# Attention on one core: half of the first image's pixels projected from whole fp32 values

## The chip, the cores and the metric

The kernel runs on one core of a Trainium2 chip. The metric is the device time of one execution in microseconds (us); lower is better.

## What is computed

Four images of 256 channels and 32 x 32 = 1024 pixels go through one attention layer. With x of one image as a 256 x 1024 matrix:

```python
q = einsum('oc,bcn->bon', Wq, xf) + bq      # 32 x 1024
k = einsum('oc,bcn->bon', Wk, xf) + bk      # 32 x 1024
v = einsum('oc,bcn->bon', Wv, xf) + bv      # 256 x 1024
attn = softmax(einsum('bqi,bqj->bij', q, k), axis=-1)
out = einsum('bcj,bij->bci', v, attn) + x
```

All tensors are fp32.

## The kernel before

**Parts.** Every fp32 operand of a matmul is cut in two: a high part of reduced precision (`x_hi`, `wqk_hi`, `wv_hi`, `v_hi`, `w_hi`, type fp32r) and the rest (`..._lo`, the value less its high part). A product is made of three matmuls into the same accumulator: high x high, low x high, high x low. Low x low is left out.

**Stages of an image.** q and k are projected together, one accumulator of 512 columns for each half of the pixels (`qk_home`); the scores of eight tiles of 128 queries are made for their row maxima and exponential sums (`first_scores`, `scores`; maxima on VectorE in `row_max`, L665, exponentials on ScalarE in `sum_exp`, L500); v is projected in eight tiles of 128 pixels x 256 channels (`v_tile`, L939); then a loop of 16 steps makes the transposed weights (`scores_t`) and multiplies v with them (`weigh_v`). In that loop the front stages of the next image are laid between the steps. The channels are two blocks of 128 (CT = 2), so each projection adds up two blocks.

**Start.** For the first image there is nothing to lay its front stages beside. The order of TensorE is written out by hand (L1078 to L1101): twenty matmuls on zeros (`keep_busy`), the q, k projection in four pieces (`first_project_qk`; piece i is channel block i // 2 and pixel half i % 2), v tiles 0 and 1, scores 0 to 2, v tiles 2 and 3, score 3, v tiles 4 and 5, the rows of shifts (`first_rows`), v tiles 6 and 7 around the first two transposed scores, then the loop, which begins with the first weighting matmul (L1009). Waits between engines are semaphores that each instruction raises when it ends; each engine runs its instructions in the order written.

**Who feeds the start.** SP's queue loads x of image 0 in two channel blocks (L278), then `wv` (L279), and after `wv` has landed x of image 1. ScalarE's queue loads `small` (L485): the q and k weights, the biases of q and k, and the bias of v. ScalarE cuts x into `x_hi` in four pieces (L487 to L490) and then `wv` into `wv_hi` (L569), and puts k and part of q with their bias (`put_k_hi`, `put_q_hi`, `put_q2_full`). VectorE cuts the weights of q and k (L624, L626) from a source that repeats each block of 32 twice, so that the accumulator holds k, k, q, q in its 128 partitions, makes `x_lo` (L632), then puts the first quarter of q (L769) and the low parts of q and k (`put_q_lo`, `put_k_lo`), then takes the four row maxima. GpSimd copies each block of the cut weights once into `wqk_pair` (L416 to L421), which the projections of images 1 to 3 use; makes `wv_lo` (L424); copies two quarters of q (`put_q_dup`); cuts and splits the second half of q (`split_q2`); then cuts and splits x of image 1 and splits the first weight tiles (`split_w`). Score 0 waits for k's low parts, q's low part and the first q copy; score 1 for q's second low part; score 2 for the second q copy; score 3 for the first exponential, since it is written over score 0; v tile 4 for the second exponential.

## Time and profile before

| | us |
|---|---|
| median of 3 executions | 163.77 |
| lowest and highest | 163.71 and 164.1 |
| the profiled execution | 163.81 |
| its span, first to last instruction | 162.0 |
| TensorE matmul busy | 157.5 (97%) |
| VectorE busy | 133.9 (83%) |
| ScalarE busy | 109.2 (67%) |
| GpSimd busy | 60.0 (37%) |

The span is counted from the first instruction recorded to the last; the execution's time holds some 1.8 us outside it. A matmul's length in a timeline includes the passage through the array, so neighbours overlap; the distance between two starts is what one costs in a row of them. The number behind an x is a count of instructions, and a bracket at the end of a row gives idle time ahead of it and what ended it. Line numbers (L849) are those of the kernel before. TensorE's operands are listed as result <- moving, stationary or the reverse, by the program's names; a product of `v_tile` is listed at L849, the line of its helper `group`, or at L948 and L952 for tile 0.

### The profile page before, as it was taken

The page shows a single profiled execution, that of the slowest core. Times are in us where ns is not written, and L with a number is a line of the kernel's source. Part 1 is how long each engine was busy: PE and PEld are TensorE (multiplying, and loading weights), DVE is VectorE, ACT ScalarE, POOL GpSimd, SP SyncE. Part 2 cuts the span into 40 slices and gives each one's busy share as a digit, 9 for nine tenths or more (in the row PEclk, how much of TensorE's full clock was granted, in tenths as well). Part 3 has the DMA queues.
Part 4 walks back from the last instruction along what each step waited for, and adds up shares of the span by engine and source line. Part 5 has one row for each costly group of instructions (what it writes and reads, how often), then busy time and mean ns, then how long its engine had stood idle before and what let it go on. Part 6 is the DMA issues. An engine that isn't in the chain of part 4 may idle for free.

```text
span 162.0 us, 2456 instructions
## 1 busy us (share of the span) xinstructions
PE 157.5 (97%) x788; PEld 132.3 (82%) x788; DVE 133.9 (83%) x215; ACT 109.2 (67%) x200; POOL 60.0 (37%) x68
## 2 busy tenths in 40 slices
PE   7999999999999999999999999999999999999993
PEld 5677887798888887798888897788888898888882
DVE  1899998888988989997989989895989779846952
ACT  3679887969999545827999646736896655756400
POOL 4479946256222316348443300342333300124500
PEclk9999999999999999999999999999999999999999
DMA  4576672152103030162711130162320330003003
GB/s 161 187 299 166 243 235 89 31 151 63 55 0 97 1 129 2 37 144 67 268 39 49 54 129 0 37 146 67 121 61 1 97 129 0 0 5 129 0 0 130
DMA packets 7780, 14.67 MB, mean 91 GB/s; under 512 B 1504, under 2 KB 2072, under 8 KB 7768
## 3 DMA queue, kind: packets, MB, share of 16 engines
q1 hardware_dynamic: 6728, 13.46, 25.4%
q0 software_dynamic: 608, 0.80, 2.2%
q10 hardware_dynamic: 432, 0.26, 0.5%
q8 instruction: 6, 0.10, 0.3%
q14 instruction: 6, 0.05, 0.1%
HBM read 4.79 MB, written 4.20 MB: 55 GB/s over the span
## 4 chain that ended last, share of the span: by engine, by line
PE 90%; DMA 2%; ACT 2%; DVE 2%; issue 1%; DVEq 0%
PE acc L1009 32%; PE acc L1015 16%; PE slot L849 11%; PE st L996 9%; PE slot L909 7%; PE slot L1009 5%; DMA small_sb<-small 2%; PE slot L1015 2%; ACT dump L504 2%; PE slot L861 2%; PE slot L866 2%; PE slot L935 1%; DVE negmax L667 1%; PE slot L881 1%; DVE x_lo L632 0%
## 5 line engine op out<-in xcount | busy, mean ns | idle before, releaser
L402 POOL TENSOR_TENSOR w_lo<-w_full,w_hi 128x512 fp32r<-128x512 f32 x21 | 28.0, 1338 | 46.6 <-ACT w_full L542 25.4
L1009 PE MATMUL acc<-w_hi,v_hi 128*128 128x512 f32 x112 | 44.3, 395 | 0.0
L1009 PE MATMUL acc<-w_hi,v_lo 128*128 128x512 f32 x112 | 44.1, 394 | 0.0
L542 ACT ACTIVATE w_full<-st 128x512 f32<-128x512 f32 x62 | 36.8, 594 | 7.6 <-PE st L996 7.5
L504 ACT ACTIVATE dump<-slot,negmax 128x1024 f32<-128x1024 f32 x29 | 32.5, 1119 | 10.5 <-DVE negmax L667 10.1
L667 DVE TENSOR_REDUCE negmax<-slot 128x1 f32<-128x1024 f32 x29 | 35.2, 1217 | 2.7 <-PE slot L909 2.7
L1015 PE MATMUL acc<-w_lo,v_hi 128*128 128x512 f32 x112 | 37.4, 396 | 0.0
L734 DVE TENSOR_TENSOR w_lo<-w_full,w_hi 128x512 fp32r<-128x512 f32 x43 | 30.7, 719 | 3.6 <-issue 0.5
L1009 PEld LDWEIGHTS acc<-w_hi,v_hi 128*128 128x128 f32 x112 | 21.1, 189 | 5.0 <-issue 0.2
L1009 PEld LDWEIGHTS acc<-w_hi,v_lo 128*128 128x128 f32 x112 | 21.2, 189 | 4.8
L1015 PEld LDWEIGHTS acc<-w_lo,v_hi 128*128 128x128 f32 x112 | 21.0, 188 | 4.8
L996 PE MATMUL st<-q_b,k_b 98*128 98x512 f32 x62 | 24.5, 398 | 0.1
L725 DVE CAST w_hi<-w_full 128x512 fp32r<-128x512 f32 x40 | 19.5, 489 | 3.0 <-ACT w_full L542 1.5
L539 ACT ACTIVATE w_hi<-st 128x512 fp32r<-128x512 f32 x24 | 14.3, 594 | 6.2 <-PE st L996 6.0
L849 PE MATMUL slot<-wv_hi,x_hi 128*128 128x256 f32 x62 | 17.4, 281 | 0.4 <-ACT dump L504 0.4
L849 PE MATMUL slot<-wv_lo,x_hi 128*128 128x256 f32 x62 | 17.4, 281 | 0.0
L849 PE MATMUL slot<-wv_hi,x_lo 128*128 128x256 f32 x62 | 17.3, 280 | 0.0
L909 PE MATMUL slot<-k_a,q_a 96*128 96x512 f32 x48 | 15.2, 397 | 0.0
L531 ACT ACTIVATE v_hi<-slot 128x512 fp32r<-128x512 f32 x12 | 7.2, 599 | 11.8 <-PE slot L849 11.8
L265 POOL DMA_DIRECT2D q_b<-shift_rows x7 | 4.2, 602 | 29.5 <-DVE shift_rows L706 27.0
L715 DVE TENSOR_TENSOR v_lo<-slot,v_hi 128x512 fp32r<-128x512 f32 x16 | 11.0, 690 | 3.8 <-ACT v_hi L531 3.7
L909 PEld LDWEIGHTS slot<-k_a,q_a 96*128 96x128 f32 x48 | 13.0, 310 | 1.1
(102 smaller groups left out, 225.2 us busy)
## 6 DMA issues: line engine op xcount, KB each, us to landing
out<-x_sb SPq DMA_DIRECT2D x7, 512.0 KB, 2.8
x_sb<-x SPq DMA_DIRECT2D x3, 1024.0 KB, 5.1
k_b<-k_a SPq DMA_DIRECT2D x8, 192.0 KB, 2.6
q_b<-q_a SPq DMA_DIRECT2D x8, 192.0 KB, 2.6
x_sb<-x SPq DMA_DIRECT2D x2, 512.0 KB, 4.2
k_a<-qk_parts SPq DMA_DIRECT2D x12, 64.0 KB, 2.0
q_a<-qk_parts SPq DMA_DIRECT2D x12, 64.0 KB, 2.2
k_a<-qk_parts POOLq DMA_DIRECT2D x6, 64.0 KB, 2.2
```

Source lines behind the costliest of these rows:

```text
L402: nc.gpsimd.tensor_tensor(w_lo[:, r, :], w_full[:, r, :], w_hi[:, r, :].bitcast(fp32), ALU.subtract).then_inc(w_split_pool, 1)
L504: nc.scalar.activation(dump[:, t % 2, :], s_home(b, t), ACT.Exp, bias=negmax[:, t:t + 1], accum_out=rowsum[:, t:t + 1]).then_inc(rowsum_re ...
L539: nc.scalar.activation(w_hi[:, r, :], st_home(n), ACT.Exp).then_inc(w_cut_act, 1)
L542: nc.scalar.activation(w_full[:, r, :], st_home(n), ACT.Exp).then_inc(exp_done, 1)
L667: nc.vector.tensor_reduce(out=negmax[:, t:t + 1], in_=s_home(b, t), op=ALU.max, axis=AX.X, negate=True).then_inc(negmax_ready, 1)
L725: nc.vector.tensor_copy(w_hi[:, r, :], w_full[:, r, :]).then_inc(w_cut_dve, 1)
L734: nc.vector.tensor_tensor(w_lo[:, r, :], w_full[:, r, :], w_hi[:, r, :].bitcast(fp32), ALU.subtract).then_inc(w_split_dve, 1)
L849: last = nc.tensor.matmul(dst, lhs, rhs, start=(i == 0), stop=(i == len(terms) - 1))
L909: last = nc.tensor.matmul(s_home(b, t)[:, cols(h)], pixels(b, t), k_a[0:K_A, cols(h)], start=True, stop=True)
L996: nc.tensor.matmul(st_home(n), k_b[0:K_B, j * P:(j + 1) * P], q_b[0:K_B, cols(h)], start=True, stop=True).then_inc(st_ready, 1)
L1009: nc.tensor.matmul(dst, v[:, b % 2, j, c * P:(c + 1) * P], w_hi[:, n % RING, part], start=(j == 0 and v is v_hi), stop=False)
L1015: return nc.tensor.matmul(dst, v_hi[:, b % 2, j, c * P:(c + 1) * P], w_lo[:, n % RING, part], start=False, stop=(j == JT - 1))
```

## The change

For the first half of the first image's pixels, q, k and v are projected by matmuls whose operands are the uncut fp32 tensors `x_sb`, `small_sb` and `wv`: one for each channel block instead of three. The second half of its pixels and all other images keep their parts; ScalarE and VectorE cut and split x of image 0 for the second pixel half only (two pieces of 512 columns each instead of four). The weights of q and k lie in `small` as k, k, q (96 columns for each channel block instead of 64), and `wqk_hi` and `wqk_lo` are 96 columns wide instead of 128. `wqk_pair` is now made by GpSimd from `small_sb` by a copy and a subtraction, behind `x0_split`; the first q copy goes ahead of `wv_lo` in GpSimd's order. TensorE runs 18 zero matmuls instead of 20, waits for `small`, takes whole and cut products in turn (block 0 whole, block 0 parts, block 1 whole, block 1 parts), waits for `wv` in place of its high part ahead of v tile 0, and for `wv_lo` ahead of v tile 4. `add_bias` on ScalarE, in the loop, waits for the v tiles of image 0 in place of its splits.

```diff
-        small_sb = sb("small_sb", [P, CT * 2 * CQK + 2 + CT])
-        bias = small_sb[:, CT * 2 * CQK:CT * 2 * CQK + 2]
-        bv_sb = small_sb[:, CT * 2 * CQK + 2:CT * 2 * CQK + 2 + CT]
-        wqk_hi = sb("wqk_hi", [P, CT, P], fp32r)
-        wqk_lo = sb("wqk_lo", [P, CT, P], fp32r)
+        KKQ = 3 * CQK
+        small_sb = sb("small_sb", [P, CT * KKQ + 2 + CT])
+        bias = small_sb[:, CT * KKQ:CT * KKQ + 2]
+        bv_sb = small_sb[:, CT * KKQ + 2:CT * KKQ + 2 + CT]
+        wqk_hi = sb("wqk_hi", [P, CT, KKQ], fp32r)
+        wqk_lo = sb("wqk_lo", [P, CT, KKQ], fp32r)
...
-            for half, (parts, made) in enumerate(((wqk_hi, wqk_cut), (wqk_lo, wqk_split))):
-                pool.wait_ge(made, 1)
-                nc.gpsimd.tensor_copy(
-                    wqk_pair[:, :, half * 2 * CQK:(half + 1) * 2 * CQK].rearrange("p c (g r) -> p c g r", g=2),
-                    parts[:, :, :].bitcast(fp32).rearrange("p c (g d r) -> p c g d r", g=2, d=2)[:, :, :, 0, :],
-                ).then_inc(pair_made, 1)
+            wqk = small_sb[:, 0:CT * KKQ].rearrange("p (c g r) -> p c g r", c=CT, g=3)[:, :, 0:3:2, :]
+
+            def pair(half):
+                return wqk_pair[:, :, half * 2 * CQK:(half + 1) * 2 * CQK].rearrange("p c (g r) -> p c g r", g=2)
+
+            pool.wait_ge(small_in, DMA)
+
+            pool.wait_ge(x0_split, CT)
+            nc.gpsimd.tensor_copy(pair(HI), wqk).then_inc(pair_made, 1)
+            pool.wait_ge(pair_made, 1)
+            nc.gpsimd.tensor_tensor(pair(LO), wqk, pair(HI).bitcast(fp32), ALU.subtract).then_inc(pair_made, 1)
             pool.wait_ge(pair_made, 2)
+            put_q_dup(0)
+            pool.wait_ge(q_dup_put, 1)
             pool.wait_ge(wv_cut, 1)
             nc.gpsimd.tensor_tensor(wv_lo[:, :, :], wv[:, :, :], wv_hi[:, :, :].bitcast(fp32),
                                     ALU.subtract).then_inc(wv_split, 1)
             pool.wait_ge(wv_split, 1)
-            put_q_dup(0)
-            pool.wait_ge(q_dup_put, 1)
             put_q_dup(1)
...
             act.preload_act_table_set("natural_log_exp_and_others")
-            for i in range(4):
-                c, part = piece(i)
+
+            for c in range(CT):
                 act.wait_ge(x0_in[c], DMA)
-                nc.scalar.activation(x_hi[:, 0, c, part], x_sb[:, 0, c, part], ACT.Copy).then_inc(x0_cut, 1)
-
+                nc.scalar.activation(x_hi[:, 0, c, cols(1)], x_sb[:, 0, c, cols(1)], ACT.Copy).then_inc(x0_cut, 1)
...
-                act.wait_ge(x0_split, 4)
+
+                act.wait_ge(v_ready, 4)
...
             dve.wait_ge(small_in, DMA)
-
-
-            def twice(w):
-                return w[:, :, :].rearrange("p c (g d r) -> p (c g) d r", g=2, d=2)
-
-            wqk = small_sb[:, 0:CT * 2 * CQK].rearrange("p (g o r) -> p g o r", o=1, r=CQK)
-            wqk = wqk.broadcast_to([P, CT * 2, 2, CQK])
-            nc.vector.tensor_copy(twice(wqk_hi), wqk).then_inc(wqk_cut, 1)
+            wqk = small_sb[:, 0:CT * KKQ].rearrange("p (c w) -> p c w", c=CT)
+            nc.vector.tensor_copy(wqk_hi[:, :, :], wqk).then_inc(wqk_cut, 1)
             dve.wait_ge(wqk_cut, 1)
-            nc.vector.tensor_tensor(twice(wqk_lo), wqk, twice(wqk_hi).bitcast(fp32),
+            nc.vector.tensor_tensor(wqk_lo[:, :, :], wqk, wqk_hi[:, :, :].bitcast(fp32),
                                     ALU.subtract).then_inc(wqk_split, 1)
-
-            for i in range(4):
-                c, part = piece(i)
-                dve.wait_ge(x0_cut, i + 1)
-                nc.vector.tensor_tensor(x_lo[:, 0, c, part], x_sb[:, 0, c, part],
-                                        x_hi[:, 0, c, part].bitcast(fp32), ALU.subtract).then_inc(x0_split, 1)
+            for c in range(CT):
+                dve.wait_ge(x0_cut, c + 1)
+                nc.vector.tensor_tensor(x_lo[:, 0, c, cols(1)], x_sb[:, 0, c, cols(1)],
+                                        x_hi[:, 0, c, cols(1)].bitcast(fp32), ALU.subtract).then_inc(x0_split, 1)
...
-            def first_project_qk(i):
-                c, part = piece(i)
-                dst = qk_home(0, i % 2)
-                if i == 0:
-                    pe.wait_ge(wqk_cut, 1)
-                pe.wait_ge(x0_cut, i + 1)
-                nc.tensor.matmul(dst, wqk_hi[:, c, :], x_hi[:, 0, c, part], start=(c == 0), stop=False)
-                if i == 0:
-                    pe.wait_ge(wqk_split, 1)
-                nc.tensor.matmul(dst, wqk_lo[:, c, :], x_hi[:, 0, c, part], start=False, stop=False)
-                pe.wait_ge(x0_split, i + 1)
-                last = nc.tensor.matmul(dst, wqk_hi[:, c, :], x_lo[:, 0, c, part], start=False, stop=(c == CT - 1))
+            def first_project_whole(c):
+
+                pe.wait_ge(x0_in[c], DMA)
+                last = nc.tensor.matmul(qk_home(0, 0)[0:KKQ, :], small_sb[:, c * KKQ:(c + 1) * KKQ], x_sb[:, 0, c, cols(0)],
+                                        start=(c == 0), stop=(c == CT - 1))
+                if c == CT - 1:
+                    last.then_inc(qk_ready, 1)
+
+            def first_project_parts(c):
+
+                dst = qk_home(0, 1)[0:KKQ, :]
+                pe.wait_ge(wqk_cut, 1)
+                pe.wait_ge(x0_cut, c + 1)
+                nc.tensor.matmul(dst, wqk_hi[:, c, :], x_hi[:, 0, c, cols(1)], start=(c == 0), stop=False)
+                pe.wait_ge(wqk_split, 1)
+                nc.tensor.matmul(dst, wqk_lo[:, c, :], x_hi[:, 0, c, cols(1)], start=False, stop=False)
+                pe.wait_ge(x0_split, c + 1)
+                last = nc.tensor.matmul(dst, wqk_hi[:, c, :], x_lo[:, 0, c, cols(1)], start=False, stop=(c == CT - 1))
...
             def v_tile(b, t):
                 px = slice(t * P, (t + 1) * P)
                 dst = v_home(b, t // VT)[:, t % VT * C:(t % VT + 1) * C]
-                terms = [(xs[:, b % 2, c, px], w[:, c, :]) for c in range(CT)
-                         for xs, w in ((x_hi, wv_hi), (x_hi, wv_lo), (x_lo, wv_hi))]
-                if b == 0 and t == 0:
-
-                    for c in range(CT):
-                        for xs in (x_hi, x_lo):
-                            nc.tensor.matmul(dst, xs[:, 0, c, px], wv_hi[:, c, :],
-                                             start=(c == 0 and xs is x_hi), stop=False)
-                    pe.wait_ge(wv_split, 1)
-                    for c in range(CT):
-                        nc.tensor.matmul(dst, x_hi[:, 0, c, px], wv_lo[:, c, :], start=False, stop=(c == CT - 1))
-                    return
+                if b or t >= TH:
+                    terms = [(xs[:, b % 2, c, px], w[:, c, :]) for c in range(CT)
+                             for xs, w in ((x_hi, wv_hi), (x_hi, wv_lo), (x_lo, wv_hi))]
+                else:
+                    terms = [(x_sb[:, 0, c, px], wv[:, c, :]) for c in range(CT)]
                 last = group(dst, terms)
...
-            keep_busy(20, QUARTER)
-            for i in range(4):
-                first_project_qk(i)
-            pe.wait_ge(wv_cut, 1)
+            keep_busy(18, QUARTER)
+            pe.wait_ge(small_in, DMA)
+            for c in range(CT):
+                first_project_whole(c)
+                first_project_parts(c)
+            pe.wait_ge(wv_in, DMA)
...
             pe.wait_ge(rowsum_ready, 2)
+            pe.wait_ge(wv_split, 1)
             v_tile(0, 4)
...
-            by_partition(np.concatenate([wk, wq], axis=0)),
+            by_partition(np.concatenate([wk, wk, wq], axis=0)),
```

## Rows read from the trace of the kernel before

**Rows 1.** Page: the span; busy time and share of TensorE.
```profile
span 162.0 us, 2456 instructions
...
PE 157.5 (97%) x788; PEld 132.3 (82%) x788; DVE 133.9 (83%) x215; ACT 109.2 (67%) x200; POOL 60.0 (37%) x68
```

**Rows 2.** By stretch: length, busy each engine, granted clock, DMA share, GB/s.
```profile
5.27:5.70 0.43, 0.43 (x3) 0.43 (x2) 0.43 (x2) 0.38 (x1) 0.43 (x2) 1.00 1.04 405
...
18.97:162.00 143.03, 140.25 (x696) 119.16 (x694) 119.77 (x191) 96.17 (x179) 46.86 (x47) 1.00 0.24 73
```

**Rows 3.** Chain of work that ended last, 0 to 26 us: start, length, what.
```profile
0.75 3.94 DMA small_sb<-small
...
11.17 1.24 DVE negmax L667
```

**Rows 4.** Timeline of PE, 0 to 23 us: start, length, line, operation, operands, count.
```profile
1.06 4.45 PE L1076 MATMUL st<-idle 128*128 128x256 bf16 x20 [1.06 <-DVE idle L614]
5.27 0.59 PE L876 MATMUL slot<-x_hi,wqk_hi 128*128 128x512 f32 x1
5.70 0.40 PE L879 MATMUL slot<-x_hi,wqk_lo 128*128 128x512 f32 x1
...
7.72 0.39 PE L881 MATMUL slot<-x_lo,wqk_hi 128*128 128x512 f32 x1
...
8.64 0.28 PE L948 MATMUL slot<-wv_hi,x_hi 128*128 128x256 f32 x1
...
10.32 0.81 PE L935 MATMUL acc<-k_a,q_a 96*128 96x512 f32 x2
...
12.18 0.28 PE L849 MATMUL slot<-wv_hi,x_hi 128*128 128x256 f32 x1
...
13.47 0.28 PE L849 MATMUL slot<-wv_hi,x_lo 128*128 128x256 f32 x1
13.69 0.74 PE L935 MATMUL acc<-k_a,q_a 96*128 96x512 f32 x2
14.82 0.38 PE L849 MATMUL slot<-wv_hi,x_hi 128*128 128x256 f32 x1 [0.39 <-ACT dump L504]
...
18.97 0.47 PE L1009 MATMUL acc<-w_hi,v_hi 128*128 128x512 f32 x1
...
22.79 0.63 PE L1015 MATMUL acc<-w_lo,v_hi 128*128 128x512 f32 x2
```

**Rows 5.** Timeline of PEld, TensorE's weight loads, 0 to 12 us.
```profile
9.50 0.19 PEld L849 LDWEIGHTS slot<-wv_hi,x_hi 128*128 128x128 f32 x1
```

**Rows 6.** Timeline of DVE, 0 to 22 us.
```profile
5.38 2.68 DVE L632 TENSOR_TENSOR x_lo<-x_sb,x_hi 128x512 fp32r<-128x512 f32 x4
8.15 0.48 DVE L769 TENSOR_SCALAR q_a<-slot,small_sb 32x256 fp32r<-32x256 f32 x1
...
9.18 1.40 DVE L642 SCALAR_TENSOR_TENSOR k_a<-slot,small_sb,k_a 32x512 fp32r<-32x512 f32 x2
...
14.57 1.22 DVE L667 TENSOR_REDUCE negmax<-acc 128x1 f32<-128x1024 f32 x1
```

**Rows 7.** Timeline of ACT, 0 to 22 us.
```profile
4.50 1.15 ACT L490 ACTIVATE x_hi<-x_sb 128x512 fp32r<-128x512 f32 x2 [2.04 <-DMA x_sb<-x]
5.82 1.15 ACT L490 ACTIVATE x_hi<-x_sb 128x512 fp32r<-128x512 f32 x2 [0.17 <-DMA x_sb<-x]
...
15.82 1.12 ACT L504 ACTIVATE dump<-acc,negmax 128x1024 f32<-128x1024 f32 x1
```

**Rows 8.** Timeline of POOL, 0 to 22 us.
```profile
5.14 0.47 POOL L418 CAST wqk_pair<-wqk_hi 128x128 fp32r<-128x128 f32 x1 [2.30 <-DVE wqk_hi L624]
...
20.92 1.29 POOL L402 TENSOR_TENSOR w_lo<-w_full,w_hi 128x512 fp32r<-128x512 f32 x1 [0.23 <-ACT w_full L542]
```

**Rows 9.** Issues of the DMA queues: issue, KB each, median us to landing.
```profile
x_sb<-x SPq DMA_DIRECT2D x2, 512.0 KB, 4.2
...
small_sb<-small ACTq DMA_DIRECT2D x1, 66.0 KB, 3.9
```

More of the change, by code:

```diff
@@ L122, in nonlocal_attention @@
         wqk_split = sem("wqk_split")
+        x0_cut = sem("x0_cut")
+        x0_split = sem("x0_split")
         pair_made = sem("pair_made")
@@ L125, in nonlocal_attention @@
         wv_split = sem("wv_split")
-        x0_cut = sem("x0_cut")
-        x0_split = sem("x0_split")
         x1_cut = sem("x1_cut")
```

## The prediction

> **What bounds the kernel now.** The first view is the busy table of the page: TensorE's matmuls cover 97% of a span of 162.0 us [rows 1]. The second is the busy time by stretch: from the first weighting matmul at 18.97 us to the end they are busy 140.25 of 143.03 us, and the change touches nothing in that stretch but one GpSimd order [rows 2]. So the time can move only by the start of that stretch, and what counts is what sets 18.97. The chain of waits tells it for the stretch before [rows 3]: the transfer of `small`, the projection of q and k on TensorE, VectorE's conversions of the first scores operands, then from 11.17 four row maxima on VectorE and four exponentials on ScalarE, back to back. The last exponential starts at 15.82 [rows 7] just behind the last maximum, which runs from 14.57 to 15.79 [rows 6]; everything up to 18.97 hangs on it. VectorE has its score 3 at 13.69 + 0.74 = 14.43, 0.14 ahead of 14.57 [rows 4, 6].
>
> **Unit prices.** Two full-speed paces come from TensorE's timeline [rows 4]. Four starts from 7.72 to 8.64 give 0.23 us for a product of 512 columns; eleven from 12.18 to 13.47 give 0.117 for one of 256. Early on the pace is slower: 20 idle products of 256 columns between 1.06 and 5.27 make 0.21 each, and the first real product holds the array from 5.27 to 5.70, 0.43 for 512 columns. That is the 1.2 GHz level, and from 5.70 on the pace is that of the 2.4 GHz level, although the granted clock of the first, slow stretch is printed as 1.00 [rows 2].
>
> **The price that no row shows** is that of a multiply on whole 32-bit values: all matmuls of the trace are on parts or on bf16 zeros. From below it is one product of its columns (0.23 or 0.117). The nearest rows are the three products of parts that it replaces (0.69 or 0.35). Two values cut in two have four products; the kernel leaves out low times low, a whole multiply can't. I take four products, 0.92 and 0.47, as the likely value. From above I let a weight load, 0.19 us long [rows 5], come bare on top of each whole multiply: 1.11 and 0.66.
>
> The Trainium skill (FP8 and Floating Point Precision, TensorE Precision Notes) gives true FP32 four passes through the array, which is the value taken. Another page of the Trainium skill (Perfetto Trace Analysis, Engine Utilization) halves the array's output rate for FP32_LOW_HIGH; read as the rate of a whole multiply, that would make it two products, the third rival below. No trace here shows either.
>
> **Part 1, q and k of image 0.** Removed are six products of parts of the first pixel half, added two whole multiplies: 12 products become 6 + 8 = 14. Two idle products go, so real work can start at 1.06 + 18 x 0.21 = 4.85 instead of 5.27. It then needs `small` and the first half of x. `small` has landed at 0.75 + 3.94 = 4.69 [rows 3], ScalarE starts on x at 4.50 [rows 7]. `small` grows from 132 to 196 columns, 66 to 98 KB. At the 405 GB/s of the stretch [rows 2] 33 KB more are 0.08 us. A 512 KB transfer landed in 4.2 us against 3.9 for this one [rows 9], so size costs little: 0 to 0.3, I take 0.08, and it hides in the 0.16 between 4.69 and 4.85. At 0.3 TensorE would start 0.14 later at the slow pace, 0.07 lost. From 4.85 to 5.70 the slow pace makes (5.70 - 4.85) / 0.43 = 2 products, the other 12 take 12 x 0.23 = 2.76, and the v tiles start at 8.46 instead of 8.64. The first half is ready when the second whole multiply drains: three products before 8.46, plus 0.16 (0.39 long less 0.23 of pace), so 7.93 against 7.72 + 0.39 = 8.11. The second half moves as much. That is 0.18 earlier for both.
>
> What feeds the second half stays behind this: ScalarE cuts two pieces instead of four, from 4.50 and, with the landing of the second half of x, from 5.82, each in some 0.6 [rows 7], and VectorE's subtraction takes 2.68 / 4 = 0.67 [rows 6], so x_lo of the second piece is there at 5.82 + 0.6 + 0.67 = 7.1, and TensorE asks for it at 8.46 - 0.23 = 8.23. Fewer weight columns (96 for 128) change no pace, since pace goes by the moving columns. The weight conversions on VectorE get shorter and wait for nothing new; they cost nothing, and are needed only from 4.85 + 0.85 + 0.46 = 6.16.
>
> **Part 2, VectorE's chain.** It started at 8.15 on the first half's projection [rows 6] and now starts at 7.97. Its second k conversion ended at 9.18 + 1.40 = 10.58, now 10.40.
>
> **Part 3, v tiles 0 and 1.** Twelve products become four whole multiplies, 16 products: 16 x 0.117 = 1.87, from 8.46 to 10.33. Before they took 8.64 to 10.32, which held a short wait for wv_lo that goes away. Score 0's first product thus starts as before; its second follows the k conversion as it did, 0.16 behind it (10.32 + 0.81 - 0.39 = 10.74 against 10.58), so at 10.56. The first row maximum moves from 11.17 to 10.99, and scores 1 and 2 move along: the next v tiles start at 12.18 - 0.18 = 12.00.
>
> **Part 4, v tiles 2 and 3.** Again 16 products for 12: 12.00 + 1.87 = 13.87. Before, score 3 came at 13.69, held by the first exponential rather than by these tiles. Now the tiles hold it: score 3 is ready at 13.87 + 0.74 = 14.61, VectorE would be free for it at 14.57 - 0.18 = 14.39. The maximum starts at 14.63 instead of 14.57. Here the 0.18 won is spent, and 0.06 more. The last exponential starts at 14.63 + 1.22 + 0.04 = 15.89 instead of 15.82, and what follows moves with it: + 0.07. Tiles 4 and 5 wait for the second exponential and had TensorE idle for 0.39 before 14.82 [rows 4], which covers the later score 3.
>
> **Part 5, GpSimd.** The pair weights were copied from 5.14 on and now wait for x_lo (7.1). They are a copy of 0.47 and a subtraction of a quarter of the size of the one that took 1.29 at 20.92 [rows 8]: 0.32 to 1.29, I take 0.32. The first q copy (no larger than the pair copy, so under 0.47) can follow at 7.97 + 0.48 = 8.45, at worst at 8.9, and is done by 9.4, before score 0 needs it at 10.33. Then comes wv_lo, at 1.3 until 10.3; nobody but tile 4 at 14.8 waits for it. Behind it are queued the second q copy, done by 10.8 and needed by score 2 near 11.5, and the long row of q and x1 pieces, which ends 0.1 to 0.9 later. Its last item that TensorE needs is the split of weight tile 1, 20.92 to 22.21, for the low product at 22.79 [rows 4, 8]: 0.23 idle before and 0.58 behind, 0.8 in all. It costs nothing at my value and 0.1 at the far end. The pairs are first used by the second image's projection, in the stretch behind 18.97. SP's transfers of the q pieces shift by the same tenths; TensorE waits for none of them before score 4, behind 18.97 too.
>
> **Sum.** The profiled execution took 163.81 us, 1.81 outside its span, and the runs shown have a median of 163.77, so no correction. 163.81 + 0.07 = 163.88, forecast 163.9.
>
> **How steep it is.** If a whole multiply costs f times four products, part 1 moves by 1.84 (f - 1), parts 3 and 4 by 1.87 (f - 1) each, with no slack left above f = 1: 5.6 (f - 1) in all. From 163.88 to 164.26 (0.3% above the median, about what a measurement of this kernel can tell from no change) is 0.38, so f = 1.07 is enough to be slower.
>
> **Rivals.**
> First, slower: a weight load of whole values isn't hidden behind the running multiply. One load of 0.19 on each of the 2 + 4 + 4 whole multiplies before score 3 is 1.9 us: 165.8; half of it 164.8. It decides from 0.04 us for each multiply on. For it: nothing here loads whole values ahead. Against it: all loads of the trace lie under a running product. Chance 0.17. The Trainium skill (TensorE: Matmul & The Clock Gate, Weight-path perf modes) keeps fast weight loading for operands that are not FP32, which speaks for this rival and names no price here.
> Second, slower: the rise to the 2.4 GHz level comes later than 5.70, as a gap or two idle products fewer might bring about. Each us at the lower level costs half of that; 1 us later gives 164.4. Against it: only some 0.1 us of gap is new. Chance 0.05.
> Third, faster: a whole multiply costs fewer than four products. With three, part 1 gains 0.46 more, parts 3 and 4 end before their gates (9.4 before 9.94, 12.94 before 13.0), the whole chain moves by 0.64: 163.2. With two, the projection waits for x_lo at 7.1, VectorE's chain starts at 7.1 instead of 8.15: 162.8. For it: only that the price isn't shown. Chance 0.10, half of it for two products.
> Fourth, the gate at score 3 doesn't bind, because a long multiply spares the per-product overhead (0.107 for 256 columns at 2.4 GHz instead of 0.117): parts 3 and 4 then lose 0.16 less each, score 3 comes 0.24 to 0.3 earlier than in the sum, and VectorE's own gain of 0.18 stands: about 163.65, still within 0.3%.
>
> **How the numbers follow.** Forecast and fourth case together 0.68, all within 0.3%. Slower 0.22 from the first and second, faster 0.10 from the third. The range of 8 in 10 takes all of the middle, the third case's upper part and the nearer half of the first: 163.3 to 164.9.
>
> **What would show it.** In the changed kernel's timeline: the first whole multiply at 4.85; its length and the next start, which price it directly; v tile 0 at 8.46; the first row maximum at 10.99; score 3 at 13.87 and the fourth maximum behind it rather than behind the third; the first weighting matmul at 19.04. A first whole multiply far from four products, a `small` that lands after 5.0, or a stretch from the first weighting to the end that isn't 143.0 us would make the prediction wrong.

## The result, and the profile after

| | before | after |
|---|---|---|
| median, us | 163.83 | 164.49 |
| lowest and highest | 163.71 to 164.1 | 164.09 to 165.1 |
| executions | 8 | 8 |
| the profiled execution and its span | 163.81, 162.0 | 164.09, 162.3 |

The ratio is 1.0039, with an interval of 1.0025 to 1.0054. The change costs 0.66 us, 0.4%. That is inside the range given, above the point forecast of 163.9, and past the 0.3% that the forecast case held. The changed kernel also scatters over 1.0 us, where the kernel before scatters over 0.4. Its profiled execution is the fastest of the eight, 0.40 under the median, so the profiles below differ by 0.28 and not by 0.66, and the start that they show need not be its usual one.

The first view to read is again the busy time by stretch, cut at the first weighting matmul, which is now at 18.33 (columns as in [rows 2]).

```profile
0.00:18.33 18.33, 16.78 (x82) 12.08 (x83) 12.88 (x22) 12.06 (x20) 11.97 (x22) 1.00 0.66 229
18.33:162.30 143.97, 140.91 (x696) 119.06 (x694) 120.75 (x192) 95.84 (x179) 46.74 (x47) 1.00 0.23 73
```

The start is 0.64 us shorter than before (18.97), where 0.07 longer was forecast. The stretch behind it, in which I had said that nothing changes, is 0.94 longer (143.97 against 143.03) with the same 696 matmuls. So there are two results to explain, of opposite sign. First the start, by the chain that ended last.

```profile
1.06 3.71 PE st L1073 x18
4.77 1.08 PE slot L871 x2
...
6.55 0.86 PE slot L871 x2
...
8.09 1.73 PE slot L847 x8
9.82 0.61 PE acc L939 x2
...
10.46 1.24 DVE negmax L665
...
11.72 1.25 ACT dump L509 x3
```

A whole multiply is recorded as two matmuls: L871 x2 is one of 512 columns, L847 x8 are four of 256. The second one of 512 columns took 0.86, one of 256 took 1.73 / 4 = 0.43. The very first took 1.08, 0.22 more: its weight load waited for `small`, with no product running beside it.

```profile
4.75 0.24 PEld L871 LDWEIGHTS slot<-x_sb,small_sb 128*96 128x96 f32 x2 [0.27 <-DMA small_sb<-small]
```

From there to 10.43 the chain has no gap, and the other whole multiplies show no weight load as idle time. The timeline of TensorE has the places that answer to [rows 4].

```profile
4.75 1.10 PE L871 MATMUL slot<-x_sb,small_sb 128*96 128x512 f32 x2
...
7.93 1.89 PE L847 MATMUL slot<-wv,x_sb 128*128 128x256 f32 x8
9.47 0.95 PE L939 MATMUL acc<-k_a,q_a 96*128 96x512 f32 x2
...
13.01 0.82 PE L939 MATMUL acc<-k_a,q_a 96*128 96x512 f32 x2
...
18.33 0.47 PE L1006 MATMUL acc<-w_hi,v_hi 128*128 128x512 f32 x1
```

Now the stretch behind 18.33. I set each matmul of after beside the same one of before and followed the difference of their starts. It is -0.64 at the first weighting, -0.40 from 22.85 on (VectorE, below, is only some 0.4 early itself), -0.30 at 49.27, and +0.20 to +0.30 from 50.70 to the end. So most of the lead is lost in one place. The timeline of TensorE there:

```profile
49.27 0.50 PE L1006 MATMUL acc<-w_hi,v_hi 128*128 128x512 f32 x1
...
50.07 0.40 PE L1006 MATMUL acc<-w_hi,v_lo 128*128 128x512 f32 x1
50.70 0.74 PE L1012 MATMUL acc<-w_lo,v_hi 128*128 128x512 f32 x2 [0.23 <-POOL w_lo L403]
```

The last two starts are 0.63 apart, where 0.23 is usual. TensorE waits for a weight tile that GpSimd splits at 49.35 (48.43 in before). GpSimd waited for ScalarE's weights, and ScalarE, earlier, for a row maximum of VectorE:

```profile
49.35 1.29 POOL L403 TENSOR_TENSOR w_lo<-w_full,w_hi 128x512 fp32r<-128x512 f32 x1 [4.67 <-ACT w_hi L545]
```

```profile
46.40 1.12 ACT L509 ACTIVATE dump<-slot,negmax 128x1024 f32<-128x1024 f32 x1 [0.92 <-DVE negmax L665]
```

Back from there stands VectorE's timeline, of after:

```profile
41.01 0.42 DVE L723 CAST w_hi<-w_full 128x512 fp32r<-128x512 f32 x1
41.92 0.69 DVE L732 TENSOR_TENSOR w_lo<-w_full,w_hi 128x512 fp32r<-128x512 f32 x1 [0.50 <-issue]
42.53 1.22 DVE L665 TENSOR_REDUCE negmax<-slot 128x1 f32<-128x1024 f32 x1
43.67 1.56 DVE L635 TENSOR_TENSOR x_lo<-x_sb,x_hi 128x512 fp32r<-128x512 f32 x1
45.16 1.21 DVE L665 TENSOR_REDUCE negmax<-slot 128x1 f32<-128x1024 f32 x1
```

and of before:

```profile
41.37 0.42 DVE L725 CAST w_hi<-w_full 128x512 fp32r<-128x512 f32 x1
41.88 0.69 DVE L734 TENSOR_TENSOR w_lo<-w_full,w_hi 128x512 fp32r<-128x512 f32 x1
42.48 1.22 DVE L667 TENSOR_REDUCE negmax<-slot 128x1 f32<-128x1024 f32 x1
43.62 0.68 DVE L637 TENSOR_TENSOR x_lo<-x_sb,x_hi 128x512 fp32r<-128x512 f32 x1
44.22 1.22 DVE L667 TENSOR_REDUCE negmax<-slot 128x1 f32<-128x1024 f32 x1
```

GpSimd's w_lo beside it, of after and then of before:

```profile
43.38 1.30 POOL L403 TENSOR_TENSOR w_lo<-w_full,w_hi 128x512 fp32r<-128x512 f32 x1 [3.16 <-PE acc L1012]
```

```profile
43.74 1.72 POOL L402 TENSOR_TENSOR w_lo<-w_full,w_hi 128x512 fp32r<-128x512 f32 x1 [3.15 <-PE acc L1015]
```

Three steps can be read off. VectorE arrives 0.36 ahead of before at 41.01, and then pauses 0.50 with nothing to wait for that the profile shows. GpSimd's subtraction is released by TensorE, which is 0.36 ahead and has no such pause, so it starts 0.29 in front of VectorE's x_lo; before it started 0.12 behind. And the one that comes second takes longer: 1.56 instead of 0.68 for VectorE in after, 1.72 instead of 1.30 for GpSimd in before. VectorE is then 0.9 late, the maximum at 49.14 instead of 48.22, and ScalarE and GpSimd behind it. The Trainium skill (SBUF — State Buffer, Who interferes with whom) says that a VectorE operation with two SBUF inputs and a GpSimd operation that reads SBUF exclude each other, and that the one that starts first holds the port for its whole length; these rows agree.

**Theory.** The pause belongs to a place in VectorE's list of instructions. Counting waits too, in order of start, it stands ahead of the 64th record of VectorE in after, and ahead of the 192nd in before (101.75, where 0.46 shows). Before's 64th record is a wait for VectorE's own cast; it starts at 40.91, while VectorE is at work on a row maximum (40.24 to 41.46) with the cast behind it, and a pause there would not show. The change takes two subtractions out of VectorE's list, so all behind them move two places up, and the 64th is now the subtraction at 41.92. The pause then turns the order of VectorE and GpSimd round. **Rivals.** The pause is a matter of time or of data, and comes with any earlier start; or the pause costs by itself and the order of the two engines nothing; or the loss comes from what the whole multiplies did to the start.

### The profile page after: what moved, and what is told of

It reads as the page before. It is cut to its first block, busy times and chain, and to the rows that moved or that the text cites. A ratio compares the mean times of both kernels' runs of the same rounds, so it can differ in the third digit from the quotient of the medians.

```text
span 162.3 us, 2431 instructions
## 1 busy us (share of the span) xinstructions
PE 157.7 (97%) x776; PEld 131.1 (81%) x776; DVE 133.6 (82%) x213; ACT 107.9 (66%) x198; POOL 58.7 (36%) x68
## 4 chain that ended last, share of the span: by engine, by line
PE 93%; DVE 2%; ACT 2%; issue 1%; DVEq 0%; ACTq 0%
PE acc L1006 31%; PE acc L1012 16%; PE slot L847 13%; PE st L993 9%; PE slot L913 7%; PE slot L1006 5%; PE slot L1012 2%; PE st L1073 2%; PE slot L859 2%; PE slot L864 2%; DVE negmax L665 1%; PE slot L939 1%; PE slot L871 1%; ACT dump L509 1%; ACT x_hi L554 0%
## 5 line engine op out<-in xcount | busy, mean ns | idle before, releaser
L847 PE MATMUL slot<-wv_hi,x_hi 128*128 128x256 f32 x56 | 15.8, 282 | 0.3 <-ACT dump L509 0.3
L847 PE MATMUL slot<-wv_lo,x_hi 128*128 128x256 f32 x56 | 15.7, 281 | 0.0
L847 PE MATMUL slot<-wv_hi,x_lo 128*128 128x256 f32 x56 | 15.7, 280 | 0.0
```

The lines of the kernel that those rows point to most:

```text
L847: last = nc.tensor.matmul(dst, lhs, rhs, start=(i == 0), stop=(i == len(terms) - 1))
```

## The experiments

**Two idle instructions on VectorE, after.** Two memsets of one column restore the places of the kernel before, and nothing else.

```diff
             nc.vector.memset(shift_parts[:, :, :].bitcast(fp32), 0.0).then_inc(zeros_put, 1)
+            for i in range(2):
+                nc.vector.memset(pad[:, i:i + 1], 0.0)
```

> The changed kernel with two one-column memsets added to VectorE's stream at 1.3 us, where VectorE is idle until 4.7. Nothing else moves. Theory (a stall in VectorE's instruction stream): the changed kernel has two VectorE instructions fewer, which moves a point of its stream at which it pauses some 0.5 us without any wait (41.43 to 41.92) from inside a wait to between two conversions; the pause makes VectorE late for GpSimd at 43.67 and TensorE then loses 0.7 us near 50. With the two instructions back the pause hides again, the conversion at 43.7 takes 0.7 instead of 1.56, and the kernel is 0.7 to 0.9 us faster than the changed one: 163.3 to 163.8, at or below the kernel before. Rival (the loss belongs to the shifted start itself, which lets GpSimd come first at 43.4 whatever VectorE's stream holds): 164.1 to 164.9 as the changed kernel.

Measured: 163.75 (163.34 to 164.37, 12 executions), against 163.88 of before beside it; ratio 0.9995 [0.9983, 1.0006], so 0.7 under after's 164.49. VectorE:

```profile
41.49 0.42 DVE L726 CAST w_hi<-w_full 128x512 fp32r<-128x512 f32 x1
42.00 0.69 DVE L735 TENSOR_TENSOR w_lo<-w_full,w_hi 128x512 fp32r<-128x512 f32 x1
...
43.74 0.68 DVE L638 TENSOR_TENSOR x_lo<-x_sb,x_hi 128x512 fp32r<-128x512 f32 x1
```

The pause is gone, x_lo is first again and takes 0.68, and TensorE's wait at 50.7 is gone. Two more instructions made the kernel faster.

**Two instructions fewer on VectorE, before.** The converse: before, with VectorE's two first memsets done by GpSimd.

```diff
+            nc.gpsimd.memset(idle[:, :], 0.0).then_inc(idle_made, 1)
...
+            nc.gpsimd.memset(shift_parts[:, :, :].bitcast(fp32), 0.0).then_inc(zeros_put, 1)
...
-            nc.vector.memset(idle[:, :], 0.0).then_inc(idle_made, 1)
-            nc.vector.memset(shift_parts[:, :, :].bitcast(fp32), 0.0).then_inc(zeros_put, 1)
```

> The kernel before with VectorE's first two memsets done by GpSimd, so that VectorE's stream is two instructions shorter, as in the changed kernel; all projections stay as before. Theory of the stream: an unexplained pause of 0.5 us appears on VectorE between its conversion and its subtraction near 41.8, the x conversion near 44 may wait for GpSimd, and the kernel is slower by 0.4 to 0.9 us: 164.2 to 164.7. Rival (the loss belongs to the whole multiplies or to the earlier start): as before, 163.7 to 163.95, plus at most 0.1 for a later start of the idle products.

Measured: 164.49 (164.42 to 164.75), ratio 1.0042 [1.0029, 1.0055].

```profile
42.23 0.69 DVE L734 TENSOR_TENSOR w_lo<-w_full,w_hi 128x512 fp32r<-128x512 f32 x1 [0.50 <-issue]
...
43.98 1.56 DVE L637 TENSOR_TENSOR x_lo<-x_sb,x_hi 128x512 fp32r<-128x512 f32 x1
```

The kernel before shows after's pause at the same instruction, the same 1.56, the same wait of 0.23 on TensorE (at 51.00) and a loss of the same size, with no whole multiply in it. So the loss needs nothing of the new projections.

**The same two memsets further back, after.** They stand behind the 64th record and ahead of the 192nd.

```diff
+                    if b == 1 and s == 0:
+                        for i in range(2):
+                            nc.vector.memset(pad[:, i:i + 1], 0.0)
```

> The changed kernel with the same two one-column memsets on VectorE, but behind the pause: at the start of the second image's loop, near 60 us. Theory of the stream: only the instructions ahead of the pause count, so the pause at 41.9 stays where it is in the changed kernel, the x conversion near 43.7 takes 1.56, and the time is that of the changed kernel, 164.1 to 164.9. Rival (two more small instructions help VectorE wherever they stand, or the gain of the padded kernel was chance): about 163.75 as the kernel padded at the front.

Measured: 164.19 (163.93 to 164.96), ratio 1.0027 [1.0014, 1.0039]; the profiled execution took 164.42. Both pauses stand where the count puts them, the first as in after, the second as in before:

```profile
42.50 0.69 DVE L733 TENSOR_TENSOR w_lo<-w_full,w_hi 128x512 fp32r<-128x512 f32 x1 [0.50 <-issue]
...
102.47 0.69 DVE L733 TENSOR_TENSOR w_lo<-w_full,w_hi 128x512 fp32r<-128x512 f32 x1 [0.46 <-issue]
```

The x_lo behind the first took 1.57, and TensorE lost 0.6 against before between 49.8 and 51.6. So it is the place, not the presence of two more instructions.

**The order forced, the pause kept, after.** GpSimd's w_lo (weight tile 11) waits for VectorE's x_lo.

```diff
                 pool.wait_ge(exp_done, n + 1)
+                if n == 11:
+                    pool.wait_ge(x_split, 1)
```

> The changed kernel with one wait more: GpSimd's subtraction for weight tile 11 (43.38 us) waits until VectorE has made the first part of x_lo of image 2 (43.67). Theory: VectorE's pause of 0.5 near 41.9 stays, but the x_lo subtraction takes 0.7 instead of 1.56, VectorE is 0.5 instead of 0.9 late behind it, and TensorE's loss near 50 falls from 0.7 to 0.3 or less: 0.4 to 0.7 us less than the changed kernel, 163.5 to 164.0. Rival (the 1.56 has another cause, or GpSimd's tile then comes late itself): no gain, 164.2 or more.

Measured: 164.0 (163.47 to 164.63), ratio 1.0007 [0.9991, 1.0024].

```profile
42.66 0.69 DVE L734 TENSOR_TENSOR w_lo<-w_full,w_hi 128x512 fp32r<-128x512 f32 x1 [0.51 <-issue]
...
44.40 0.68 DVE L637 TENSOR_TENSOR x_lo<-x_sb,x_hi 128x512 fp32r<-128x512 f32 x1
```

The pause is there, x_lo takes 0.68, and TensorE shows no wait near 50: its distance to before is +0.35 at 23.60 and never moves by more than 0.06 from there on. That +0.35 was made ahead of the loop and in its first steps (first weighting matmul at 19.12, 0.15 late). So in the profile the pause alone costs nothing here, and the order costs the 0.5 to 0.6. The medians are less sharp: 164.0 is 0.25 above the first experiment's 163.75, with intervals that overlap, so a small cost of the pause is not excluded.

**The same two memsets, before.** The first experiment's two memsets, put in at the same place of the kernel before.

```diff
             nc.vector.memset(shift_parts[:, :, :].bitcast(fp32), 0.0).then_inc(zeros_put, 1)
+            for i in range(2):
+                nc.vector.memset(pad[:, i:i + 1], 0.0)
```

> The kernel before with the two one-column memsets added in the same place. A control: the instructions cost nothing where they stand (VectorE is idle there). Theory of the stream: the pause moves two instructions ahead, to just before or in the row maximum at 40.2, where VectorE has no wait to hide it, so up to 0.5 us of VectorE and 0 to 0.5 us of the whole: 163.8 to 164.3. Rival (position in the stream means nothing): 163.7 to 163.95.

Measured: 164.32 (164.24 to 164.37), ratio 1.0026 [1.0016, 1.0036], slower. The loss is at another place. TensorE:

```profile
36.73 0.63 PE L1018 MATMUL acc<-w_lo,v_hi 128*128 128x512 f32 x2
37.74 0.82 PE L912 MATMUL slot<-k_a,q_a 96*128 96x512 f32 x2 [0.39 <-DMA k_a<-qk_parts]
```

The scores of image 1 wait for a transfer of k's parts, and SP's next transfer starts at 37.37 instead of 36.65. Two transfers of 8 KB by an instruction queue, at 37 and 41 in before, lie at 35 and 37 here, but why the transfer lands late I can't show. The pause that I expected two instructions ahead shows nowhere on VectorE, at neither of the two places. This run says that two instructions more are no cure as such; its own loss stays unexplained.

**One part of the change alone: v.** Before, with v tiles 0 to 3 whole and all else in parts.

```diff
+                    terms = [(x_sb[:, 0, c, px], wv[:, c, :]) for c in range(CT)]
```

> The kernel before with one part of the change alone: v tiles 0 to 3 of image 0 from whole values, q and k still in parts, 20 idle products, GpSimd's order and VectorE's number of instructions as before. By the whole multiply's measured price (1.73 us for eight instructions, four times 256 columns at 2.4 GHz each, so 1.71 for two tiles against 1.41 in parts) v tiles 2 and 3 end 0.2 later than score 3 started before, of which VectorE has 0.14 in hand: 0.05 to 0.1 slower, 163.85 to 164.05. Rival (whole multiplies are themselves the loss of the changed kernel): 164.2 or more.

Measured: 163.79 (163.68 to 164.88), ratio 1.0001 [0.9987, 1.0014]. TensorE:

```profile
8.71 1.89 PE L850 MATMUL slot<-wv,x_sb 128*128 128x256 f32 x8
...
19.04 0.47 PE L1003 MATMUL acc<-w_hi,v_hi 128*128 128x512 f32 x1
```

Whole v tiles alone are worth nothing and cost nothing that can be told: VectorE's chain still starts where q and k let it, and the first maximum is at 11.23 (before 11.17).

**The other part alone: q and k.** After, with v in parts, for which ScalarE and VectorE cut and split all four pieces of x again. GpSimd makes the pair weights early again and the first q copy behind `wv_lo`, as in before.

```diff
-                nc.scalar.activation(x_hi[:, 0, c, cols(1)], x_sb[:, 0, c, cols(1)], ACT.Copy).then_inc(x0_cut, 1)
+                for h in (1, 0):
+                    nc.scalar.activation(x_hi[:, 0, c, cols(h)], x_sb[:, 0, c, cols(h)], ACT.Copy).then_inc(x0_cut, 1)
...
-                    terms = [(x_sb[:, 0, c, px], wv[:, c, :]) for c in range(CT)]
```

> The other part of the change alone: q and k of the first pixel half from whole values and 18 idle products, but the v tiles in parts, so ScalarE and VectorE cut and split all four pieces of x again, the second pixel half first. VectorE's stream has as many instructions as in the kernel before, so the pause hides. VectorE's q and k chain starts at 7.85 or later instead of 8.15, v tile 0 waits for wv_lo until 9.2, score 0 starts near 10.2. Theory: a gain of 0.1 to 0.4 against the kernel before, less dependent on when TensorE's clock rises than the changed kernel: 163.4 to 163.8. Rival (the whole v tiles are what makes the change worth trying): 163.9 or more.

Measured: 164.91 (164.87 to 165.08), ratio 1.0065 [1.0053, 1.0077], slower where I had thought it faster. VectorE, then GpSimd:

```profile
8.26 0.48 DVE L770 TENSOR_SCALAR q_a<-slot,small_sb 32x256 fp32r<-32x256 f32 x1
...
16.00 1.19 DVE L675 CAST shift_parts<-negmax 128x4 fp32r<-128x4 f32 x1
```

```profile
15.88 1.28 POOL L413 TENSOR_TENSOR x_lo<-x_sb,x_hi 128x512 fp32r<-128x512 f32 x1
```

A cast of 4 columns, 0.17 elsewhere, starts 0.12 behind a GpSimd subtraction and takes 1.19, until that ends. TensorE's rows of shifts come at 17.50 instead of before's 16.41, and the first weighting matmul at 19.85. It is the same collision at another place, with twice the price. Beside it VectorE's chain starts at 8.26, no earlier than before's 8.15, since it splits four pieces again, in 2.85, and TensorE waits 0.40 for wv_lo at 9.41. Those are the two things that whole v tiles spare when q and k are whole.

**GpSimd moved out of the way, two forms.** Both start from the first experiment and let GpSimd's cast of x1 wait for the shift (it costs VectorE 0.3 there, 0.47 instead of 0.17). The first form then puts weight tile 1 behind x1's last split; the second puts it ahead.

```diff
+            pool.wait_ge(shift_ready, 1)
             cut_x1(1)
             split_x1(1)
             pool.wait_ge(x1_split, 2)
-
-            pool.wait_ge(shift_ready, 1)
             cut_x1(2)
             split_x1(2)
             pool.wait_ge(x1_split, 3)
-            cut_x1(3)
-            pool.wait_ge(x1_cut, 4)
 
             split_w(1)
+            pool.wait_ge(w_split_pool, 1)
+            cut_x1(3)
+            pool.wait_ge(x1_cut, 4)
```

> The changed kernel with the two memsets at the front, and GpSimd's work on x of image 1 kept off VectorE's first shift conversions: the second cut waits until the shifts are made, and the fourth cut goes behind the split of weight tile 1. In the padded kernel VectorE's 128x4 conversion at 15.80 took 0.47 instead of 0.20, until GpSimd's cut ended at 16.24. Theory (the two engines exclude each other for such operations): it takes 0.2 again, TensorE's row matmuls start 0.2 to 0.3 earlier and the first weighting too: 163.4 to 163.6, 0.2 to 0.3 less than the padded kernel. Rival (GpSimd's later tile 1 then holds TensorE, or the rows weren't on the path): 163.7 or more.

Measured: 164.16 (163.72 to 164.85), ratio 1.0023 [1.0009, 1.0036]. VectorE:

```profile
16.13 0.17 DVE L675 CAST shift_parts<-negmax 128x4 fp32r<-128x4 f32 x1
...
19.73 1.48 DVE L735 TENSOR_TENSOR w_lo<-w_full,w_hi 128x512 fp32r<-128x512 f32 x1
```

The 0.3 is won at 16.13. The delayed row of GpSimd then has its x_lo run at 19.36 for 1.30, ahead of VectorE's w_lo, and TensorE waits 0.42 for that at 21.27. A collision moved, not removed.

```diff
+            pool.wait_ge(shift_ready, 1)
             cut_x1(1)
...
-            pool.wait_ge(shift_ready, 1)
             cut_x1(2)
+            pool.wait_ge(x1_cut, 3)
+
+            split_w(1)
+            pool.wait_ge(w_split_pool, 1)
             split_x1(2)
...
-            split_w(1)
```

> The changed kernel with the two memsets at VectorE's front and GpSimd's early work laid between VectorE's: the second cut of x of image 1 waits for the first shifts, the third subtraction and the fourth cut go behind the split of weight tile 1. In the run before this one (GpSimd late) the shift conversion took 0.17 as hoped, but GpSimd's third subtraction then ran from 19.36 to 20.66 and VectorE's subtraction for weight tile 0, due at 19.73, took 1.48. Theory: without an overlap at 15.8 or at 19.7 both take their usual 0.2 and 0.7, and the kernel is 0.2 to 0.4 us faster than the one with the memsets alone in the median: 163.3 to 163.6, faster than the kernel before. Rival (GpSimd's reordered pieces meet VectorE elsewhere, near 23, or the median follows TensorE's early pace alone): 163.7 or more.

Measured: 163.49 (163.28 to 164.1), ratio 0.9982 [0.9972, 0.9993]. VectorE's shift cast at 15.44 takes 0.17 and its w_lo at 19.04 takes 0.68; two operations at 22.53 and 23.51 take 0.88 and 0.91 instead of 0.4 and 0.7. This version is faster than both kernels, by 0.18% of before and 1.0 us of after.

**Twenty idle products again.** The first experiment's kernel with the 20 of before.

```diff
-            keep_busy(18, QUARTER)
+            keep_busy(20, QUARTER)
```

> The changed kernel with the two memsets at VectorE's front and 20 idle products instead of 18. Theory: with whole multiplies TensorE works without a gap from the last idle product to score 0, so two idle products (0.21 us each at the slow pace, 0.11 at the fast one) push everything: 0.2 to 0.4 us later at v tile 0 than with 18, 0.1 to 0.3 in the median: 163.85 to 164.1. Rival (the start is held by the transfers or by VectorE, not by TensorE): 163.75 as with 18.

Measured: 163.57 (163.21 to 164.34), ratio 0.9994 [0.998, 1.0008]; the 163.85 to 164.1 that I expected isn't there. Its profiled execution started early in spite of more idle products, which leads to the clock. The first whole multiply in the timelines of this kernel and of the first experiment's:

```profile
1.06 3.77 PE L1076 MATMUL st<-idle 128*128 128x256 bf16 x20 [1.06 <-DVE idle L621]
4.80 1.10 PE L874 MATMUL slot<-x_sb,small_sb 128*96 128x512 f32 x2
```

```profile
1.06 4.02 PE L1076 MATMUL st<-idle 128*128 128x256 bf16 x18 [1.06 <-DVE idle L621]
4.88 1.57 PE L874 MATMUL slot<-x_sb,small_sb 128*96 128x512 f32 x2
```

The same multiply took 1.10 and 1.57. Twenty idle products took 3.77 here and eighteen 4.02 there. In the one the pace doubled, from the 1.2 GHz level (0.21 for an idle product) to the 2.4 GHz level (0.11), while the idle products ran, in the other after them. The granted clock is printed as 1.00 throughout.

## Why the prediction was right and wrong

**The sentence that the change touches nothing behind 18.97 but one GpSimd order failed, and it decided the result.** The prediction looked in the loop for waits that the change moves, found that order, and costed it at nothing (part 5). For the item itself that held: weight tile 1's split ran from 20.38 to 21.67, and TensorE's low product came at 22.34. What it didn't count is that two VectorE instructions leave the list and a pause of 0.50 moves with the count, from under running work to open ground; nor that VectorE's x_lo and GpSimd's w_lo stood 0.12 apart in before with nothing to hold their order. Before alone showed both, the 0.46 ahead of 101.75 and the GpSimd row of 1.72 among rows of 1.30. With the two places given back the change measures 163.75 [0.9983, 1.0006], near the 163.88 of the sum; with only the two places taken, before measures 164.49, as much as after. In the profiles the loop took 140.86 from the first weighting to the last matmul in after, 139.96 in before and 139.86 in the first experiment. Of the 1.0 between the last and the first, 0.60 falls between 49.3 and 51, some 0.17 ahead of it, and 0.23 in steps of 0.02 to 0.04 up to 144, which I did not trace.

That 164.49 lies inside the range is luck: the room above the forecast was made for bare weight loads and a late clock, and the loss came from the loop. By its own last sign, a stretch that isn't 143.0 (it was 143.97), the account fails though the number holds.

**Unit price, partly wrong: 0.92 and 0.47 were taken, 0.86 and 0.43 came.** Those are 8 and 4 x 0.107 (256 columns at 2.4 GHz), four products without the overhead of 0.01 to 0.02 that each product of parts has. This is the fourth case's price. The first case (bare weight loads), to which most of the slower chance was given, didn't happen, but for the 0.22 of the very first multiply, which had no product ahead of it to hide behind: that the time came near the 164.8 of its half form has another reason. The third (fewer than four products) is out. The Trainium skill (FP8 and Floating Point Precision, TensorE Precision Notes) agrees with its four passes. The halved rate of the Trainium skill (Perfetto Trace Analysis, Engine Utilization) holds only if read for each of the two recorded matmuls, 0.43 for 512 columns: the whole is four products, not two.

**Part 1, start: 4.85 said, 4.75 measured, v tile 0 at 8.46 said, 7.93 measured.** `small` landed in 4.0 us instead of 3.9, as the value of 0.08 had it. Of the 0.53, 0.10 is the earlier start, about 0.12 the price (two multiplies, 0.06 each) and the rest the clock: two slow products from 4.85 to 5.70 were in the sum, which cost 0.40 more than two fast ones, and this execution had none. In the first experiment's profile, where the clock rose late, v tile 0 is at 8.53.

**Part 2 and Part 3** follow: VectorE's chain began at 7.45 instead of the 7.97 said, and the first maximum at 10.46 instead of 10.99. With the late clock (first experiment) it is 11.06. The chain of causes held; its date was the clock's.

**Part 4, the gate at score 3, failed.** Forecast were score 3 at 13.87, held by the v tiles, and the fourth maximum behind it. The tiles do hold score 3: they drain at 11.47 + 1.89 = 13.36, and the first exponential (11.72 and 1.25 long) has ended at 12.97. Its row starts at 13.01 because its first product is listed beside the last tile's. But its two products end at 13.01 + 0.82 = 13.83, and the maxima stay back to back, the fourth at 13.87. The sum had score 3 ready 0.22 behind VectorE (14.61 against 14.39); it was 0.04 ahead. Of these 0.26, 0.14 is the price, 1.73 for what was costed at 1.87, as the fourth case said, and some 0.11 comes from the 0.74 that was taken for score 3: behind the tiles' last product (13.36 less a passage of 0.16) it took 13.83 - 13.20 = 0.63. Even with v alone whole the fourth maximum moved by 0.07 only.

**What wasn't said of the start:** of the 0.64 won at the first weighting matmul 0.24 was back at 22.85. VectorE's shift split waited for GpSimd's cast of x1:

```profile
15.41 0.47 DVE L674 TENSOR_TENSOR shift_parts<-negmax,shift_parts 128x4 fp32r<-128x4 f32 x1
```

and GpSimd for comparison:

```profile
15.24 0.61 POOL L409 CAST x_hi<-x_sb 128x512 fp32r<-128x512 f32 x1
```

VectorE was thus 0.43 ahead of before and TensorE met it at the first w_lo. It is the collision of the loop in small, and no row of before that I read held it.

**The second rival, the clock,** was seen as a risk of a later rise. What the runs show is a start that in the changed kernels hangs on the rise at all. In the three profiles with q, k and v in parts (before and the two variants of it) v tile 0 starts between 8.60 and 8.64 whenever the pace rose. In the seven with q, k and v whole it starts anywhere from 7.93 to 8.87 and the first weighting matmul from 18.33 to 19.20. That fits the wider scatter of the changed kernels; each run has one profile, so the link to the times is argued, not shown. Whether 18 or 20 idle products have a part in when the pace rises stays open: two kernels' medians, 163.75 and 163.57, don't tell it.

## What to carry to other kernels

Before a kernel is changed ahead of a tight loop, count how many instructions each engine's list gains or loses, look in the trace of before for idle time ended by "issue", and ask which instruction will stand there. List the places where VectorE and GpSimd both read SBUF within some tenths of a us of each other, and which one is first: a small lead turned round costs the short operation the whole rest of the long one, far from the edit. When a gain of the expected size doesn't reach the end, follow the difference between equal matmuls of the two traces along time; it names the place in one pass.

## What the runs showed of the hardware

**VectorE pauses 0.46 to 0.51 us at fixed places of its list:** ahead of the 64th and the 192nd record, so 128 apart, in eleven of the twelve profiles at one of them and in one of these at both; adding or removing two instructions ahead of a place moved the pause by two. Where none shows, VectorE was at work or waited for something else. One transfer of 8 KB by an instruction queue lies close by, in after between 42.5 and 43:

```profile
DMA packets 1, 0.01 MB, mean 16 GB/s; under 512 B 0, under 2 KB 0, under 8 KB 0
## 3 DMA queue, kind: packets, MB, share of 16 engines
q14 instruction: 1, 0.01, 4.0%
```

In before one starts between 41.0 and 41.25, and one behind the pause at 101.75, between 102.3 and 103. Both transfers next to a visible pause start some 0.7 after the pause has ended (41.92 and 101.75), so VectorE did not wait for these to land. That the pause has to do with the fetch of instructions is argued from the distance and the nearness, not shown. The Trainium skill (Runtime: NRT & Kernel Launch, Instruction fetch mechanics) has refills in 16 KiB blocks of 256 instructions, mostly hidden; by its size of an instruction the 8 KB here would be 128 (an estimate), the distance between the two places. Here the pause stayed unseen only where VectorE was at work or waiting.

**VectorE and GpSimd held each other up** where both read SBUF: a 4-column cast lasted 1.19 for 0.17, 512-column subtractions of VectorE 1.48 to 1.57 for 0.68, and one of GpSimd 1.72 for 1.30. In each the engine that started later waited. A 4-column cast that took 0.47 in the first experiment took 0.17 when GpSimd was moved away. The cited page of the Trainium skill says the same of the subtractions, which have two SBUF inputs; casts it lists among the operations that can contend.

**A whole fp32 multiply** took 0.86 for 512 columns and 0.43 for 256, four passes of its columns without the overhead between them. Behind other products its weight load showed no idle time; the first one, with nothing running ahead of it, took 1.08.

**The pace of TensorE rose between 3.9 and over 5.7 us** after the start in programs that begin alike: in before with the two memsets the idle products come 0.11 apart from there on, and with the order forced the first half of the first whole multiply still takes 0.87 (4.88 to 5.75) for 0.43. The granted clock is printed as 1.00 in both.
